# A graph kernel's second layer: its mix work moved into the loop that gathers edge rows

## The reference

```python
xn   = layernorm(x)
mean = segment_sum(xn[src], dst) / max(deg, 1)                        # over the edges
out  = mean @ W_l.T + b_l + xn @ W_r.T                                # then normalized: gnn
qkv  = (xn @ w_qkv + b_qkv)                                           # 8 heads of 3 x 32
k, v = layernorm(k), layernorm(v)                                     # per head
kv   = einsum('bhnd,bhne->bhde', k, v) / N                            # over all nodes
ret  = einsum('bhnd,bhde->bhne', q, kv) + xn
mix  = gelu(ret @ w1 + b1) @ w2 + b2 + xn
x    = x + gnn + mix
```

## Time and profile before

| | us |
|---|---|
| Time of the runs (median of 3; lowest, highest) | 6528.96 (6525.89 to 6530.78) |
| The profiled execution, its own time | 6524.86 |
| Its span (first to last instruction) | 6523.2 |
| POOL, PE, DVE, ACT busy in it | 3694.9, 3916.1, 3514.9, 677.8 |
| TensorE's mean granted clock | 0.829 |

### The profile page before, as it was taken

How to read it: one execution, slowest core, us unless ns; L and a number is a source line. 1 busy time by engine, 2 the same in 40 slices (tenths; PEclk the granted TensorE clock), 3 DMA queues, 4 the chain that set the end, 5 groups by cost and what they waited for, 6 DMA issues and landing times. The chain is left out here.

```text
span 6523.2 us, 84837 instructions
## 1 busy us (share of the span) xinstructions
PE 3916.1 (60%) x18036; PEld 2960.0 (45%) x18037; DVE 3514.9 (54%) x7152; ACT 677.8 (10%) x1606; POOL 3694.9 (57%) x3921
## 2 busy tenths in 40 slices
PE   0005666266640599899766676767677766317990
PEld 0004555154420599688544444444444444316770
DVE  9999999742223588824344444444444425731113
ACT  3000000212210000222100000000000002202320
POOL 1777777777777782000477777777777730051006
PEclk9999999999855799999777777777777768558995
DMA  3333333333333698100333333333333350111114
GB/s 94 103 103 102 99 100 102 100 101 98 102 102 102 235 333 301 59 1 6 105 103 104 103 104 103 103 104 103 103 103 103 104 57 2 61 68 64 63 61 125
DMA packets 382410, 666.59 MB, mean 102 GB/s; under 512 B 207743, under 2 KB 235991, under 8 KB 369671
## 3 DMA queue, kind: packets, MB, share of 16 engines
q0 software_dynamic: 148768, 375.57, 19.6%
q1 hardware_dynamic: 233575, 290.24, 15.3%
HBM read 519.29 MB, written 146.21 MB: 102 GB/s over the span
## 5 line engine op out<-in xcount | busy, mean ns | idle before, releaser
L1628 POOL DMA_INDIRECT rows<-projected_rows,pw_in x1664 | 1619.8, 973 | 989.4 <-issue 488.6
L576 POOL DMA_INDIRECT rows_by_src<-ring,stage x1563 | 1515.1, 969 | 484.6 <-issue 454.9
L1786 PE MATMUL pg<-rows,hot 128*125 128x256 f32 x3328 | 1279.4, 525 | 661.8 <-DMA rows<-projected_rows,pw_in 518.1
L1786 PEld LDWEIGHTS pg<-rows,hot 128*125 128x125 f32 x3328 | 764.7, 253 | 1160.9 <-issue 1057.9
L1644 DVE TENSOR_TENSOR agg<-agg,pg 125x256 f32 x832 | 349.1, 420 | 890.0 <-PE pg L1786 880.9
L1101 PE MATMUL pw<-hot,win 128*128 128x125 f32 x3968 | 453.1, 277 | 277.6 <-DVE hot L1045 274.9
L1101 PEld LDWEIGHTS pw<-hot,win 128*128 128x128 f32 x3968 | 448.3, 193 | 283.0 <-issue 282.4
L1693 DVE SCALAR_TENSOR_TENSOR hot<-pw_in,m_block_first,g_numbers 128x250 f32<-128x250 int32 x832 | 391.2, 470 | 296.7 <-issue 229.3
L808 PE MATMUL phist<-hi,lo 128*125 128x50 bf16 x3136 | 413.8, 281 | 219.3 <-DVE hi L608 219.3
L808 PEld LDWEIGHTS phist<-hi,lo 128*125 128x125 bf16 x3136 | 370.5, 222 | 264.0 <-issue 257.0
L1045 DVE SCALAR_TENSOR_TENSOR hot<-win,win_base,iota_f 128x1000 f32<-128x1000 f32 x248 | 340.5, 1373 | 137.2 <-POOL acc L1001 128.1
(11 more groups left out here) (422 smaller groups left out, 5933.2 us busy)
## 6 DMA issues: line engine op xcount, KB each, us to landing
win<-rows_by_src SPq DMA_DIRECT2D x248, 516.0 KB, 5.0
ring<-in_edge_attr SPq DMA_DIRECT2D x97, 1024.0 KB
rows<-projected_rows,pw_in POOLq DMA_INDIRECT x1664, 2.8
rows_by_src<-ring,stage POOLq DMA_INDIRECT x1563
XT<-moe_rows SPq DMA_DIRECT2D x56, 256.0 KB
moe_results<-XT POOLq DMA_DIRECT2D x56, 256.0 KB, 2.3
pw_in<-pairs_by_dst SPq DMA_DIRECT2D x832, 2.0 KB
e_w<-in_L_ffn_W SPq DMA_DIRECT2D x16, 512.0 KB
```

What stands on the lines that cost most here:

```text
L576: pool.indirect_dma_start(rows_d, bass.IndirectOffsetOnAxis(ap=stage[:, h * HC + j:h * HC + j + 1].bitcast(U32), axis=0), ring4[:, h, j, : ...
L1628: pool.indirect_dma_start(rows[:, (2 * (s % RU) + r) * D:(2 * (s % RU) + r + 1) * D], None, proj_d, bass.IndirectOffsetOnAxis(ap=pw_in[:, ...
L1786: mm = pe.matmul(pg[0:P, s % 4, 0:D], hot[:, ((s % 4) * 2 + r) * P:((s % 4) * 2 + r + 1) * P], rows[:, (2 * (s % RU) + r) * D:(2 * (s % RU ...
```

## The change

1. **The gather block takes over all of the mix.** Key and value tiles go two to an iteration (one in each half of eight windows), so that 25 iterations hold all 50. Iteration 25 folds the weights: PE at windows 4, 8 and 12, DVE at 6, 10 and 14. Iterations 26 to 50 each carry one group of two feed-forward tiles: PE `hidden` at window 1 and `second` at 6 and 11 (b2 is added there by a product with ones), ACT gelu, DVE `add_y` at 8 and 13 with three operations a tile. Iteration 51 is plain. The two mix blocks go. Buffers are shared (the fold's weights lie in wn, kn, w_self and wkv; the hidden values in kv), and SP loads the weights after its first 16 pairs.
2. **The scatter block is unrolled** on DVE, ACT, PE and SP: `each_tile` in place of `tiles`, ranking with one semaphore, one-hots with five buffers in place of two. POOL's list stays as it is.
3. `row_stats_loop` is unrolled, in both places that use it.
4. `at` no longer counts up its second semaphore where the value is a constant.

```diff
@@ at
     eng.wait_ge(sem, value)
-    eng.sem_inc(passed)
+    if not isinstance(value, int):
+        eng.sem_inc(passed)
@@ row_stats_loop
-        with dve.Fori(0, NT // 2) as i:
-            for u in range(2):
-                ins = dve.bn_stats(stats[:, bass.ds((i * 2 + u) * 6, 6)], read(i * 2 + u))
-            ins.then_inc(stats_done, 1)
+        for t in range(NT):
+            ins = dve.bn_stats(stats[:, t * 6:(t + 1) * 6], read(t))
+            if t % 2:
+                ins.then_inc(stats_done, 1)
@@ scatter block (and so for max_k, q_softmax, out_stats, add_mix, store_xt, exps, store_out, transpose_x, k_transposed, qkv, attend)
+    def each_tile(body, n=NT):
+        for t in range(n):
+            body(t, t % 2, t // 2)
-            tiles(dve, norm, ch, 6)
+            each_tile(norm)
@@ gather block, DVE
-                if s == 8:
-                    if not isinstance(t, int):
+                if s == 4:
+                    if not first(t):
                         at(dve, ctx_done, t, passed["dve"])
                     dve.tensor_tensor(by_group, by_group, hm[:].unsqueeze(2).to_broadcast([P, 16, HD]), ALU.subtract).then_inc(kv_c, 1)
-                if s == 10:
+                if s == 5:
                     at(dve, sq_ready, t + 1, passed["dve"])
...
+            def add_y(t):
+                ch.step(dve.tensor_scalar(xn, Rt(t), mean[:, bass.ds(t, 1)], rstd[:, bass.ds(t, 1)], ALU.subtract, ALU.mult))
+                ch.step(dve.tensor_tensor(Rt(t), Rt(t), xn, ALU.add))
+                at(dve, y_ready, t + 1, passed["dve"])
+                dve.tensor_tensor(Rt(t), Rt(t), pv[0:P, 0, 0:D], ALU.add).then_inc(y_added, 1)
...
-                    if tile:
-                        norm_kv(i, s)
-                    if tile and s == V_AT:
-                        add_own(i, i * U + s - 1)
+                    if part == "tiles":
+                        t = i * 2 + s // HALF
+                        if s % HALF == 4:
+                            add_own(t, i * U + s - 1)
+                        norm_kv(t, s % HALF)
+                    if part == "fold":
+                        fold(s)
+                    if part == "mix" and s in (8, 13):
+                        add_y((i - MIXED) * 2 + (s == 13))
@@ gather block, PE
+            def hidden(g):
+                if not first(g):
+                    at(pe, h_stored, g * 2, passed["pe"])
+                for m in range(2):
+                    for k in range(2):
+                        mm = pe.matmul(pk[:, 0, m * GC:(m + 1) * GC].rearrange("p (t c) -> p t c", t=2), wp[:, k * D + m * 128:k * D + (m + 1) * 128],
+                                       XTg(g, k), start=(k == 0), stop=(k == 1))
+                mm.then_inc(h_ready, 1)
...
-                    if tile and s == 4:
-                        project(i)
-                    if tile and s == 6:
-                        project_own(i)
-                    if tile and s == 15:
-                        context(i)
+                    if part == "tiles":
+                        t = i * 2 + s // HALF
+                        if s % HALF == 0:
+                            if not first(t):
+                                context(t - 1)
+                            project(t)
+                        if s % HALF == 1:
+                            project_own(t)
+                    if part == "fold":
+                        if s == 0:
+                            context(NT - 1)
+                        fold(s)
+                    if part == "mix":
+                        if s == 1:
+                            hidden(i - MIXED)
+                        if s in (6, 11):
+                            second(i - MIXED, int(s == 11))
...
-            windows(0)
-            with pe.Fori(1, NT) as i:
-                windows(i)
-            with pe.Fori(NT, NW2 // U) as i:
-                windows(i, tile=False)
+            windows(0, "tiles")
+            with pe.Fori(1, TILED) as i:
+                windows(i, "tiles")
+            windows(FOLD, "fold")
+            pe.wait_ge(fold_dve, 3)
+            windows(MIXED, "mix")
+            with pe.Fori(MIXED + 1, MIXED + G) as i:
+                windows(i, "mix")
+            for i in range(MIXED + G, NW2 // U):
+                windows(i)
```

More of the change, by code:

```diff
@@ L644, in rank_chunk @@
[L644 to L655 removed]
+                out = pos_f[:, lo:lo + n]
@@ new lines, in rank_chunk, with step, after, mask_block @@
+                at_step = {}
+                def step(kind, b, ins):
+                    ins.then_inc(rank_step, 1)
+                    rank_steps[0] += 1
+                    at_step[kind, b] = rank_steps[0]
+                def after(*ops):
+                    seen = [at_step[op] for op in ops if op in at_step]
+                    if seen:
+                        dve.wait_ge(rank_step, max(seen))
+                def mask_block(b):
+                    after(("place", b - 4))
+                    step("mask", b, dve.tensor_scalar(masks[:, b % 4, 0:n], hi_src[:, lo:lo + n], iota_f[:, b:b + 1], None, ALU.is_equal))
@@ new lines, in scan_block, with place_block @@
+                def scan_block(b):
+                    after(("mask", b), ("place", b - 4), ("carry", b - 4))
+                    step("scan", b, dve.tensor_tensor_scan(pqkv[:, b % 4, 0:n], masks[:, b % 4, 0:n], pctx[:, 0, 0:n], first_src[:, b:b + 1],
+                                                           ALU.add, ALU.bypass))
+                def place_block(b):
+                    after(("scan", b), ("place", b - 1))
+                    step("place", b, dve.copy_predicated(out, masks[:, b % 4, 0:n].bitcast(U16), pqkv[:, b % 4, 0:n]))
+                    step("carry", b, dve.tensor_copy(first_src[:, b:b + 1], pqkv[:, b % 4, n - 1:n]))
@@ L753, in add_mix @@
                 ch.step(dve.scalar_tensor_tensor(out=Rt(t), in0=b_sum[:], scalar=deg_out[:, bass.ds(t, 1)], in1=Rt(t), op0=ALU.mult, op1=ALU.add))
[L755 removed]
+            each_tile(add_mix)
         @block.scalar
@@ L1740, in _, with mix @@
                 parts(i)
+            def mix(g):
+                if not first(g):
+                    at(act, y_ready, 2 * g, passed["act"])
+                at(act, h_ready, g + 1, passed["act"])
+                for m in range(2):
+                    act.activation(hT[:, m * GC:(m + 1) * GC], pk[:, 0, m * GC:(m + 1) * GC], ACT.Gelu, bias=bp[:, m:m + 1]).then_inc(h_stored, 1)
+            act.wait_ge(fold_dve, 3)
+            mix(0)
+            with act.Fori(1, G) as i:
+                mix(i)
         @block.tensor
```

424 lines of the change are left out of this document (157 added, 267 removed).

## The result

The kernel after takes 6333.26 us (median of 4 runs, 6330.18 to 6336.44), the kernel before on the same chip 6527.99 us (4 runs). The ratio is 0.9701, 95% interval 0.9685 to 0.9718. The profiled execution of after took 6333.92 us with a span of 6332.2 us, so between the two profiled executions lie 190.9 us. The prediction had 163.6 us: the sign and the main term held, and the time came out 32 us under the forecast and 9 us under the low end of the range. 27 of the 32 us are the larger gain between the profiled executions, and 4 us are what the forecast had put on top of its sum for the median.

A forecast was written before the change was run, and what follows sets the result against it. The prediction took POOL's issue of indirect DMAs in the scatter and gather blocks as the bound. 6524.86 - 166.8 + 3 + 3 - 0.7 - 2.1 = 6361.3 us, 4.1 us under the runs' median, so 6365 us, range 6345 to 6385 (68%).

The forecast's parts named there:

- What bounds the kernel, and what goes: Scatter and gather blocks: POOL's DMA issue sets the pace; mix moved beside the gather removes 166.8 us, if all is covered.
- DVE carries it: Gather block: a second tile leaves DVE some 9 us of its 17 us wait for PE; not the new bound.
- PE carries it: Gather block: two tiles and 16 windows take PE 38.9 us on average against POOL's iteration of 40.9 us; it fits.
- The +3 us: Gather iteration heads: PE at low clock is 8.2 us late against 5 us slack; 3 us taken, between 0 and 75.
- the 17% for a drag between 6385 and 6440: Rival, gather iteration heads: clock stays low over some, POOL loses 1 to 3 us in each of 25 iterations; 17%.
- DVE slows POOL's DMAs: Gather block: DVE products of two SBUF operands lengthen gathers; moved but same number, so 0, 15 us either way.
- the tiles' operations meet fewer DMAs: Rival, gather block: the tiles' operations meet fewer DMAs, 15 to 30 us less, time 6335 to 6350; 4%.
- `add_y`: Gather block: its new operation with two SBUF operands a tile slows POOL's DMAs; +3 us, between 0 and 20.
- the rival's 21 us: Rival, gather block: `add_y`'s `tensor_scalar` bars POOL for its own length, some 0.42 us, 50 times; 21 us added, 6386; 5%.
- The scatter block: Scatter block: unrolling's savings fall into a 100 us gap nobody waits for; only the first ranking gains, 0.7 us.
- The statistics loop: Before the experts: straight code costs less an instruction than the loop, and this copy is on the path; -2.1 us.
- the signs that the prediction named: Seam within 1 us, plateau 2142 within 20, 0.97 us a DMA, DVE's wait some 600, clock above 0.75, scatter's last 2159.

The follow-up runs named there:

- a_project3_3: The kernel after with each key and value tile's projection done three times over: 6337.71 us, ratio 0.9694 to the kernel before.
- b_pause_4: The kernel before with a VectorE copy added ahead of two of the products: 6500.40 us, ratio 0.9957.
- a_roll_2: The kernel after with the scatter block, the statistics loop and `at` as before: 6346.00 us, ratio 0.9722 to the kernel before.
- b_unroll: The kernel before with only the unrolled scatter block, the straight statistics loop and the dropped semaphore counts: 6517.16 us, ratio 0.9970.

## Why the prediction was right and where it was wrong

- **What bounds the kernel, and what goes.** Right. POOL's pace set the block, and the seam shrank from 167.95 us to 0.74 us.
- **DVE carries it.** Right in kind. The tiles' stretch has 595.3 us of VectorE's work in 25 iterations, 23.8 us each, where 923.7 us in 50 were 18.5 before. Its wait for PE there is 223.1 us, 8.9 an iteration, where the prediction had 9. The whole fell only to 790.3 us and not to 600, because the iterations without tiles wait some 20 us each, where 17 was the mean before.
- **PE carries it.** Right, with two terms mis-sized. The sum for an iteration was 38.9 us and is 29.8: some 22 us for the windows instead of 25.1, and 8.1 for the two tiles instead of 13.8. The clock is the smaller part of this. At 0.80 instead of 0.75 the prediction's two sums give 36.5 us, and the same way of adding up gives 32.0 us for the kernel before, whose trace has 28.6. It priced a tile at the low level at twice 4.6 us, and in after, from the second tile on, no head takes more than 6.8 us, with a window's sum within it. The other term is the heads. The +3 us, and the 17% for a drag between 6385 and 6440, hung on a PE that is 8.2 us late with 5 us of slack. Neither happened: a head of 6.8 us is 2.8 us late by the same count, and the check that follows is a late one, since the one at window 8 wants only the first four windows summed. So POOL's margin stays above 5.8 us in after, and a_project3_3 spends 2 to 4 us of it with one wait of 1.4 us.
- **DVE slows POOL's DMAs.** The step that failed is "the change moves these operations but keeps their number, so I take 0". The prediction saw that the cost "depends on how they meet" and gave it +-15 us. It didn't go back to the trace of before, where the rule stood in the rows: the earlier trace rows shows a product that starts 0.14 us ahead of a gather, and the cases with 0.95 us start behind it. Measured: -11.1 us with `add_y` in it, so 14 us away from the forecast's 0 + 3, and b_pause_4 moves 28 us by phase alone. The rival "the tiles' operations meet fewer DMAs", at 4%, is what happened in kind, though it had 15 to 30 us.
- **`add_y`.** +3 us was taken, 5.0 us measured, 4.0 of them under the two-operand L1663: right. The `tensor_scalar` L1662 of after was under 19 gathers' starts and cost 1.0 us in all, 0.13 us at most. Eight of these gathers started 0.15 to 0.18 us into it and waited for its end; the nine that started within its first 0.13 us were not held. So it doesn't bar POOL for its length, and the rival's 21 us fall. The Trainium skill ("SBUF — State Buffer", Who interferes with whom) says that a VectorE operation with two inputs in SBUF contends with a GpSimd instruction that reads SBUF, and gives as inferred that generating a DMA's descriptors is not hurt by it. The trace agrees with the first part, if an indirect DMA's start counts as such a read (that it is the read of its indices is a guess that no run shows); it contradicts the second for this kind of DMA, by up to 0.52 us each.
- **The scatter block.** "All that the unrolling saves on DVE, ACT and PE goes into a 100 us gap that nobody waits for" is right for their lists. What failed is the silence about POOL's own pace in it: the same collisions happen there. The scatter and the statistics together were worth 12.7 us by a_roll_2 and 12 to 27 us by b_unroll, not 2.8.
- **The statistics loop.** -2.1 us forecast, and 18.6 us became 16.4: right.

Of the 27 us by which the gain was larger, 14 are the gathers' collisions, 3 the heads that cost nothing, 2 shorter waits in the last 64 gathers, 4 the scatter's DMAs and some 4 small pieces outside. The first and the fourth are phase; that the profiled pair got this much of it is luck. Over all the traces above, the scatter's last DMA came 5 us earlier in the mean of the unrolled ones, and 8.5 us from a_roll_2 to after.

Of the signs that the prediction named, these came: the next block starts 0.3 us after the last add's end, the plateau (2128.5 us) is within 20 us of 2142, its mean gather takes 0.967 us, the clock is above 0.75. Two did not: VectorE's wait for PE, and the scatter's last DMA, which moved from 2159.6 to 2154.9 us.

## What to carry to other kernels

When an engine sets the pace by issuing indirect DMAs, look up what VectorE runs at the start of the long ones. If it has two operands in SBUF, put one in PSUM before anything else: here it was worth 34 us without a single operation less. Two loops that wait for each other can keep their phase, so an edit that only moves work can gain or lose the sum of all such collisions; bound it from zero up to every one caught. And read the slack of a ring off the trace, from the end of the work that a check wants to the start of what it releases, at the check that follows the late piece.

## What the runs showed of the hardware

- In these traces an indirect DMA of POOL that starts 0.05 us or more into a VectorE operation with two SBUF operands waits for its end (0.95 us become up to 1.47 us); one that starts 0.02 us ahead of it doesn't. Where both start within some 0.04 us, the operation is the longer one (0.69 us become 0.75). An operand in PSUM takes the effect away altogether (0.97 us at most in 1664 gathers).
- The clock granted to TensorE was higher with more work an iteration: 0.75 with one tile, 0.80 with two, 0.91 with three projections each.
- Executions exist in which PE and VectorE run their lists at a fraction of the pace beside POOL's DMAs: one matmul in 2 to 3.5 us instead of eight in 1.6 us, until the DMAs end. The whole kernel takes 32% longer, and the worth of an edit is another one: the unrolled list some 300 us instead of 13 to 20, the mix beside the gather 27 us instead of 167.
